# Graph layers and routed experts on one core: work merged around the two graph sums, a selection moved off VectorE, attention items that begin at their first edge

## The chip, the cores and the metric

The kernel runs on one core of a Trainium2 chip. The metric is the device time of one execution in microseconds (us), median of several runs. Everything lies in one launch; all data are float32.

## The reference, cut to what matters

```python
def _layernorm(x): return (x - mean(x)) / sqrt(var(x) + 1e-5)      # rows of 256
...
# x is (6250, 256); 200000 edges sorted by dst, in one of 8 relations each
x = x + relation_layer(_layernorm(x))      # sum over edges of (x @ weight[type])[src] * 0.5**0.5 + h_bias + loop part
x = x + experts(_layernorm(x))             # gates from attention over 131072 + 8192 edges
x = x + selected_layer(_layernorm(x))
x = x + slice_attention(_layernorm(x))     # 8 heads, 64 slices
...
# experts: leaky-relu attention logits, segment softmax over dst, scores, top 2 of 4, softmax
for ei in range(4):
    hh = gelu(x @ W1[ei] + b1[ei])
    out = out + g[..., None] * (hh @ W2[ei] + b2[ei])
...
# selected_layer
h_self, h_neigh = feat @ W_self, feat @ W_neigh
h_sparse = h_neigh with all but the 32 largest of each row at zero
neigh = segment_sum(h_sparse[src], dst) / maximum(deg, 1.0)[:, None]
return h_self + neigh
...
# slice_attention
slice_weights = softmax((x_mid @ W_slice + b_slice) / clip(temperature, 0.1, 5.0))
out_x = slices attended, spread back by slice_weights
return out_x.reshape(B, N, INNER) @ W_out + b_out
```

## The kernel before, in words

The 6250 rows of x lie in SBUF as 49 windows of 128 rows (`b.x`, in the profile `features`, 128x12544 elements). Beside it stands the accumulator `b.acc` (in the profile `big`), 257 columns a window: 256 sums and a count. The program is a row of stages, each a `Phase` with its own code for every engine, closed by a barrier over all engines. Inside a stage engines wait for one another by semaphores only; VectorE (DVE), ScalarE (ACT), TensorE (PE), GpSimd (POOL) and SyncE (SP) run their instructions in the order written. So that order is the whole schedule: nothing is planned at build time.

The stages around the change:

- `relation_sums` (L839) gathers rows of the edges by GpSimd, multiplies them by one-hot places on TensorE and adds the sums on VectorE. `far_edges` does nothing for these inputs.
- `add_relations` (L1585) sets `degree` and adds `acc * 0.5**0.5` (L1602) and the bias `h_bias` (L1606) to x, each in one VectorE instruction over all windows.
- `row_statistics` (L374) of "ln2": 49 `bn_stats` (L397) and a few small steps make mean and rstd.
- `edge_items` (L1974) cuts the sorted attention edges into items of at most 128 edges of one window. It counts per window (L2037, L2039), sums over windows on TensorE (L2074), finds each item's window (L2043, L2045) and tile (L2047), and GpSimd gathers the keys of nine times 128 items (L2023). An item here is an aligned tile of 128 edges together with a window that it touches: a tile on the border of two windows is two items. VectorE then splits the keys (L2055 to L2058), TensorE turns them, and `esrc_items`, `edst_items` and `near_items` are made (L2061 to L2069).
- `attention_inputs`, `far_peaks`, `attention_rows`, and then `attention_edges` (L2105): a turn treats TURN = 8 items. `MAIN` = 848 places for items give 106 turns; the first `UNITS` = 100 turns stand beside one expert unit of TensorE each, the last six stand alone, two of them before a hardware loop, two in it and two behind it. A turn builds one-hot places (L2281), takes the target's terms (L2288), waits for GpSimd's gathers of the sources (L2236), makes logits (L2308) and parts (L2319), and TensorE adds them (L2375). Were there more items than `MAIN`, the flag `a.over` (L2042) would send `far_peaks` (L1736) through its loops over all items and windows.
- `gates` (L2421; its first instruction on VectorE is L2469).
- `blend` (L2529): per window SyncE loads the four experts' outputs (128x4x256, 512 KB) into one of 6 slots, ScalarE makes four diagonals of the gates (L2561), TensorE multiplies each diagonal with an expert's output and sums in PSUM (L2571, `m_mixed`), VectorE adds that to x (L2583) and counts (L2579).
- `sparse_table` (L2592): ScalarE normalizes (L2734) and copies products of both weights out of PSUM into `n_full` (L2754), GpSimd adds the self part to x (L2662), VectorE finds the 32 largest by four rounds of `max` (L2678) and `match_replace` (L2681) over groups of four windows, 8 windows in a ring, and multiplies where the marker stands (L2687) into `n_sparse`, which is stored.
- `neighbour_sums` and `far_edges`, then `add_neighbours` (L2758): the reciprocal of `degree` (L2768), `acc * share` (L2770), its addition to x (L2773), each over all windows; `row_statistics` of "ln4"; `slice_weights` (L2817): loads, TensorE products of two weights, and their scaling by the temperature (L2855, L2861, L2864).
- `slice_tokens`, `slice_attention`, and `slice_output` (L3160): ScalarE copies a window of the slice weights (L3176), TensorE multiplies it (L3185), VectorE adds to x (L3194), SyncE stores.

## Time and profile before

| | us |
|---|---|
| median of 3 runs | 6084.98 (6080.4 to 6094.47) |
| the profiled execution's own time | 6074.39 |
| its span in the profile | 6072.7 |
| TensorE busy | 4259.9 |
| GpSimd busy | 3332.0 |
| VectorE busy | 2604.2 |
| ScalarE busy | 1712.5 |

Where the touched stages lie in the span, by the first and last instruction of their lines:

| stage | from us | to us |
|---|---|---|
| add_relations, ln2, edge_items | 2414.8 | 2492.7 |
| last six attention turns, to the next stage | about 4046 | 4108.2 |
| blend | about 4135 | 4227.9 |
| sparse_table | about 4232 | about 4408 |
| add_neighbours, ln4, slice_weights | 5634.7 | 5712.3 |
| slice_output | 5980.3 | 6072.7 |

A busy share is an average over all stages. What a change to one stage is worth is read from the windows and the timeline of that stage. In a row of the timeline the bracket holds the idle time of the engine just before the instruction and what ended it; "remote" is an event whose source the profile does not name. A row with "xN" stands for N instructions in a row, its duration for all of them.

### The profile page before, as it was taken

The numbers are of one execution on the slowest core, as the hardware profiler recorded it, in microseconds if no ns is written. First come the engines' busy times: TensorE is split into PE (matmuls) and PEld (weight loads), VectorE is DVE, ScalarE is ACT, GpSimd is POOL, SyncE is SP. The second block draws the span as 40 slices with busy tenths as digits, with TensorE's granted clock in tenths as the row PEclk, the third lists the DMA queues.
The fourth block names the chain that finished last, engine by engine and source line by source line (L and its number), as shares of the span: only waits on it lengthen the run. The fifth ranks groups of instructions, "written<-read, shape, count | busy, mean of one in ns | idle before, by whom it ended". The sixth has DMA issues, their size and how long they took to land. (4 is left out here: it accounts for less than half of the span.)

```text
span 6072.7 us, 74083 instructions
## 1 busy us (share of the span) xinstructions
PE 4259.9 (70%) x18413; PEld 3046.3 (50%) x18414; DVE 2604.2 (43%) x8618; ACT 1712.5 (28%) x3921; POOL 3332.0 (55%) x3370
## 2 busy tenths in 40 slices
PE   5888877645555554467777777756668888888498
PEld 2455446333333333445555555545246666666366
DVE  7655424333333332433333333334944443443682
ACT  3344330000000000123333333325365543443132
POOL 5777665666666665055555555551256666666121
PEclk9999998776667766577878888878889999999698
DMA  6444442433333333122222122216144444443001
GB/s 219 154 158 156 158 155 79 130 92 93 91 92 92 92 96 82 14 70 43 43 41 44 40 44 42 42 34 191 41 147 144 138 121 121 121 121 115 16 1 43
DMA packets 331160, 564.00 MB, mean 93 GB/s; under 512 B 75064, under 2 KB 231365, under 8 KB 324507
## 3 DMA queue, kind: packets, MB, share of 16 engines
q0 software_dynamic: 141088, 319.86, 19.9%
q1 hardware_dynamic: 189789, 240.92, 12.6%
q8 instruction: 110, 1.80, 0.1%
q14 instruction: 173, 1.42, 0.1%
HBM read 461.01 MB, written 99.50 MB: 92 GB/s over the span
## 5 line engine op out<-in xcount | busy, mean ns | idle before, releaser
L990 POOL DMA_INDIRECT e_ring<-table,erow x1040 | 990.1, 952 | 523.4 <-issue 267.2
L1290 PE MATMUL e_sums<-e_ring,e_onehot 128*128 128x257 f32 x2080 | 772.2, 518 | 626.6 <-issue 351.5
L2236 POOL DMA_INDIRECT t_source<-source_rows,t_index x848 | 804.3, 948 | 717.9 <-DVE t_parts L2319 476.5
L1401 POOL DMA_INDIRECT e_ring<-table,esrc x800 | 791.2, 989 | 424.2 <-issue 207.3
L1290 PEld LDWEIGHTS e_sums<-e_ring,e_onehot 128*128 128x128 f32 x2080 | 494.0, 257 | 889.9 <-issue 570.8
L585 POOL DMA_INDIRECT r_ring<-rows,esrc x528 | 584.4, 1107 | 239.8 <-issue 131.8
L2395 PE MATMUL t_out<-t_w,t_hidden 128*128 128x256 f32 x1600 | 526.8, 459 | 172.3 <-issue 166.8
L1477 PE MATMUL e_total<-e_loads,e_times 128*128 128x256 f32 x2176 | 577.4, 397 | 47.7 <-issue 36.9
L2395 PEld LDWEIGHTS t_out<-t_w,t_hidden 128*128 128x128 f32 x1600 | 345.6, 225 | 308.6 <-issue 263.1
L1477 PEld LDWEIGHTS e_total<-e_loads,e_times 128*128 128x128 f32 x2176 | 413.3, 198 | 138.6 <-issue 64.7
L1488 PE MATMUL e_sums<-e_ring,e_onehot 128*128 128x256 f32 x1600 | 432.8, 393 | 48.7 <-DMA e_ring<-table,esrc 31.6
L1195 DVE SCALAR_TENSOR_TENSOR big<-e_sums,within,big 128x257 f32 x130 | 63.0, 484 | 875.4 <-DMA r_ring<-rows,esrc 740.9
L2385 PE MATMUL t_raw<-big,t_w 128*128 (+1 forms) x1600 | 426.4, 425 | 7.3 <-issue 5.4
L931 ACT ACTIVATE d_half<-d_keys 128x512 f32<-128x512 f32 x105 | 62.7, 597 | 1204.8 <-issue 614.3
L756 PE MATMUL r_sums<-r_ring,r_onehot 128*128 128x257 f32 x1056 | 300.0, 400 | 134.6 <-DMA r_ring<-rows,esrc 67.6
L742 PE MATMUL r_product<-weights,r_xt 128*128 128x512 f32 x784 | 387.3, 620 | 0.8 <-ACT r_stage L795 0.8
L1424 DVE TENSOR_SCALAR e_place<-e_rampw,ddst 128x512 bf16<-128x512 f32 (+2 forms) x768 | 285.7, 414 | 226.6 <-remote 157.8
L1488 PEld LDWEIGHTS e_sums<-e_ring,e_onehot 128*128 128x128 f32 x1600 | 315.9, 199 | 105.2 <-issue 54.4
L2385 PEld LDWEIGHTS t_raw<-big,t_w 128*128 128x128 f32 x1600 | 334.8, 215 | 61.6 <-issue 10.2
L1382 ACT ACTIVATE e_times<-e_tally 128x512 f32<-128x512 f32 (+2 forms) x384 | 177.8, 463 | 594.1 <-remote 445.9
L756 PEld LDWEIGHTS r_sums<-r_ring,r_onehot 128*128 128x128 f32 x1056 | 196.8, 196 | 286.2 <-issue 180.1
L2281 DVE TENSOR_SCALAR t_place<-t_ramp,near_items 128x128 bf16<-128x128 bf16 x848 | 148.1, 259 | 412.4 <-remote 411.6
(447 smaller groups left out, 6371.8 us busy)
## 6 DMA issues: line engine op xcount, KB each, us to landing
table<-r_stage SPq DMA_DIRECT2D x49, 1024.0 KB
e_loads<-table SPq DMA_DIRECT2D x384, 128.0 KB
t_near<-near_rows SPq DMA_DIRECT2D x106, 256.0 KB
m_outputs<-first_outputs SPq DMA_DIRECT2D x49, 512.0 KB, 4.9
first_outputs<-t_stage SPq DMA_DIRECT2D x96, 256.0 KB
e_ring<-table,erow POOLq DMA_INDIRECT x1040
t_source<-source_rows,t_index POOLq DMA_INDIRECT x848
e_ring<-table,esrc POOLq DMA_INDIRECT x800
```

The costliest lines, as they stand in the source:

```text
L585: eng.indirect_dma_start(ring[:, t % RING, 0:D], None, m["rows1"], bass.IndirectOffsetOnAxis(ap=b.esrc[:, t:t + 1], axis=0)).then_inc(gath ...
L742: mm = eng.matmul(product[n % BANKS][:, :], xt[w % 2][:, k, :], b.weights[:, k, 2 * c:2 * c + 2, :].rearrange("p r o -> p (r o)"), start=( ...
L756: eng.matmul(sums[g % 2][:, 0:ACCW], onehot[t % RING][:, :], ring[:, t % RING, :], start=(t % EGROUP == 0), stop=(t % EGROUP == EGROUP - 1 ...
L990: eng.indirect_dma_start(ring[:, t % BODY, 0:D], None, table, bass.IndirectOffsetOnAxis(ap=b.erow[:, EARLY + t:EARLY + t + 1], axis=0)).th ...
L1290: eng.matmul(sums[g % SUMS][:, 0:ACCW], onehot[t % ONEHOTS][:, :], ring[:, t % BODY, :], start=(t % GROUP == 0), stop=(t % GROUP == GROUP ...
L1401: eng.indirect_dma_start(ring[:, t % BODY, :], None, table, bass.IndirectOffsetOnAxis(ap=b.esrc[:, FROM + t:FROM + t + 1], axis=0)).then_i ...
L1424: eng.tensor_scalar(place[tile % MARKS][:, 0:wide(g) * P], rampw[:, 0:wide(g) * P], b.ddst[:, column(tile):column(tile) + 1], None, ALU.is ...
L1477: mm = eng.matmul(into[:, q, :], times[g % TIMES][:, q * P:(q + 1) * P], loads[:, g % AHEAD, :], start=False, stop=False, skip_group_check ...
L1488: eng.matmul(sums[g8 % 2][:, 0:D], onehot[t % ONEHOTS][:, :], ring[:, s, :], start=(t % GROUP == 0), stop=(t % GROUP == GROUP - 1)).then_i ...
L2236: eng.indirect_dma_start(source[s][:, q, :], None, a.source_rows, bass.IndirectOffsetOnAxis(ap=index[s][:, q:q + 1], axis=0)).then_inc(gat ...
L2385: mm = eng.matmul(raw[g][:, j % 2, :], w1[:, e, k, j * P:(j + 1) * P], b.xt[:, k, bass.ds(w * P, PAIR)], start=(k == 0), stop=(k == KH - 1))
L2395: mm = eng.matmul(out[s][:, q, :], hidden[s][:, j, q * P:(q + 1) * P], w2[:, e, j, :], start=(j == 0), stop=(j == NB - 1))
```

## The change

**Around the first sum.** The bias is loaded in `relation_sums` and added to x there by seven instructions `lift(j)`, one to each run of 7 windows. `add_relations`, the "ln2" statistics and `edge_items` become one stage, `joined_items`: VectorE adds the sums run by run (`join`), counts run by run (`tally`), and the steps of the items stand between.

```diff
+            def lift(j):
+                eng.wait_ge(restored, 16)
+                eng.wait_ge(offset, 16)
+                eng.tensor_tensor(b.x[:, RUN * j:RUN * (j + 1), :], b.x[:, RUN * j:RUN * (j + 1), :],
+                                  bias[:, :].unsqueeze(1).broadcast_to([P, RUN, D]), ALU.add).then_inc(biased, 1)
...
+                if t in bias_at:
+                    lift(bias_at.index(t))
...
+            def join(j):
+                run = b.x[:, RUN * j:RUN * (j + 1), :]
+                eng.scalar_tensor_tensor(run, b.acc[:, RUN * j:RUN * (j + 1), 0:D], 0.5 ** 0.5, run,
+                                         ALU.mult, ALU.add).then_inc(joined, 1)
+            def tally(j):
+                eng.wait_ge(joined, j + 1)
+                for w in range(RUN * j, RUN * (j + 1)):
+                    eng.bn_stats(stats[:, w, :], b.x[:, w, :]).then_inc(tallied, 1)
...
+            join(0)
+            eng.wait_ge(edged, 16)
+            step(eng.tensor_scalar(part[:, :], edge[:, :].bitcast(F32), limit[0:NW, 0:1].bitcast(F32), None, ALU.is_lt))
+            step(eng.tensor_reduce(inner[:, :], part[:, :], AX_X, ALU.add))
+            step(eng.scalar_tensor_tensor(end[:, :], counted[0:NW, 0:1], float(P), inner[:, :], ALU.mult, ALU.add))
+            step(eng.tensor_scalar(laid[:, :], b.ident[0:NW, 0:NW], end[:, 0:1], None, ALU.mult))
...
+            for j in range(EARLIER):
+                join(j + 1)
+                tally(j)
             eng.wait_ge(gathered, 16 * GROUND)
             step(eng.tensor_scalar(word[:, :, :], keys[:, :, :], 8191, None, ALU.bitwise_and))
...
+            for j in range(EARLIER, RUNS):
+                if j + 1 < RUNS:
+                    join(j + 1)
+                tally(j)
...
+            s = Chain(eng, stated)
+            variances(eng, s, b, stats, work)
             eng.wait_ge(turned, 1)
```


VectorE in `joined_items`, before: the two additions, the statistics (49, in a loop), then the items up to the keys' first step (`i_word`).

```order
L1601 TENSOR_SCALAR degree<-big 128x49
L1602 SCALAR_TENSOR_TENSOR features<-big,features 128x12544
L1606 TENSOR_TENSOR features<-features,a_bias 128x12544
L113 UNCONDITIONAL_BRANCH
L391 UNCONDITIONAL_BRANCH
L394 UNCONDITIONAL_BRANCH
L394 ISA
L397 ISA
L397 BN_STATS ln_stats<-features 128x6
```

And VectorE there in the changed kernel, shortly behind the item tiles (`i_tile`, L2120) to the keys' first steps.

```order
L2125 CAST i_windowt<-i_counted 9x128
L2127 TENSOR_TENSOR i_columni<-i_column 9x128
L2073 SCALAR_TENSOR_TENSOR features<-big,features 128x1792
L2079 BN_STATS i_stats<-features 128x6 x7
L2073 SCALAR_TENSOR_TENSOR features<-big,features 128x1792
L2079 BN_STATS i_stats<-features 128x6 x7
L2073 SCALAR_TENSOR_TENSOR features<-big,features 128x1792
L2079 BN_STATS i_stats<-features 128x6 x7
L2073 SCALAR_TENSOR_TENSOR features<-big,features 128x1792
L2079 BN_STATS i_stats<-features 128x6 x7
L2133 TENSOR_SCALAR i_word<-i_keys 128x1152
L2134 CAST i_src<-i_word 128x1152
```


What was ahead of the items' start now stands between the tiles (`i_tile`), which release the gathers, and the keys (`i_word`), which wait for them; run 0 is joined before the tiles, in the wait for the gather of `i_edge`.

**Items begin at a window's first edge.** A window's edges are cut from its own first edge on, not at aligned tiles, so only its last item is short. GpSimd first gathers one row of 128 edges per window (`i_edge`), by which VectorE finds where each window ends; a prefix sum over windows in six doublings gives the items' starts, and the nine gathers of keys use element offsets. `MAIN` becomes 816: 102 turns, of which two stand alone behind the 100 units, in straight code. With the reference's inputs there are 810 items (832 by the old cut).

```diff
-MAIN = -(-(GT * N // GSPACE + NW + 16) // TURN) * TURN
+MAIN = -(-(GT * N // GSPACE + NW // 2 + 10) // TURN) * TURN
...
+            eng.indirect_dma_start(edge[:, :], None, b.sorted, bass.IndirectOffsetOnAxis(
+                ap=whole[:, 0:1], axis=0)).then_inc(edged, 16)
...
             for g in range(GROUND):
-                eng.indirect_dma_start(keys[:, g, :], None, b.sorted, bass.IndirectOffsetOnAxis(
+                eng.indirect_dma_start(keys[:, g, :], None, anywhere, bass.IndirectOffsetOnAxis(
                     ap=tile[:, g:g + 1], axis=0)).then_inc(gathered, 16)
...
+            for k in range(6):
+                reach = 1 << k
+                v.did(eng.tensor_copy(starts[1 - s][:, 0:reach], starts[s][:, 0:reach]))
+                step(eng.tensor_tensor(starts[1 - s][:, reach:NW], starts[s][:, reach:NW], starts[s][:, 0:NW - reach], ALU.add))
+                s = 1 - s
+            start = starts[s]
             v.did(eng.tensor_scalar(a.over[:, :], start[0:1, NW - 1:NW], float(MAIN), None, ALU.is_gt))
             step(eng.tensor_tensor(passed[:, :, :], item[:, :].unsqueeze(2).broadcast_to([P, GROUND, NW]),
...
-            step(eng.tensor_reduce(window[:, :], passed[:, :, :], AX_X, ALU.add))
-            step(eng.tensor_tensor(item[:, :], item[:, :], window[:, :], ALU.subtract))
-            eng.tensor_scalar(tile[:, :], item[:, :], float(GT), None, ALU.min).then_inc(tiled, 1)
...
+            step(eng.tensor_reduce(first[:, :], weighed[:, :, :], AX_X, ALU.add))
+            step(eng.scalar_tensor_tensor(first[:, :], item[:, :], float(P), first[:, :], ALU.mult, ALU.add))
...
-            for t in range(UNITS, LEAD):
-                body(t, t % 2, None, None)
-            with eng.Fori(0, (TURNS - 2 - LEAD) // 2) as i:
-                for n in range(2):
-                    body(2 * i + LEAD + n, (LEAD + n) % 2, None, None)
-            for t in (TURNS - 2, TURNS - 1):
+            for t in range(UNITS, TURNS):
```


**Blend.** VectorE adds the fourth expert (`gate`), one window ahead; ScalarE and TensorE treat three.

```diff
+                wait_if(eng, gated, w - SLOTS + 1)
                 eng.dma_start(outputs[w % SLOTS][:, :, :], first[w]).then_inc(fetched[w % SLOTS], 16)
...
+                for e in range(TURNED):
                     eng.activation(gates[w % BANKS][:, e, :], b.ident[:, :], ACT.Copy,
...
+            def gate(w):
+                eng.wait_ge(fetched[w % SLOTS], 16 * (w // SLOTS + 1))
+                eng.scalar_tensor_tensor(b.x[:, w, :], outputs[w % SLOTS][:, TURNED, :], a.gate[:, w, TURNED:EXPERTS],
+                                         b.x[:, w, :], ALU.mult, ALU.add).then_inc(gated, 1)
...
             for w in range(NW):
+                if w + 1 < NW:
+                    gate(w + 1)
                 eng.wait_ge(summed, w + 1)
+                eng.wait_ge(gated, w + 1)
                 eng.tensor_tensor(b.x[:, w, :], b.x[:, w, :], mixed[w % BANKS][:, 0:D], ALU.add).then_inc(blended, 1)
```


VectorE in the blend, changed kernel (before, a window had L2583 and L2579 alone: the addition of `m_mixed` and the statistics).

```order
L2672 SCALAR_TENSOR_TENSOR features<-m_outputs,gate,features 128x256 x2
L2685 TENSOR_TENSOR features<-features,m_mixed 128x256
L2672 SCALAR_TENSOR_TENSOR features<-m_outputs,gate,features 128x256
L2685 TENSOR_TENSOR features<-features,m_mixed 128x256
L2677 BN_STATS counts<-features 128x6
```


Each window has an instruction more on VectorE, and it stands before the wait for TensorE's sum of the window ahead.

**Selection.** The marker of taken values is now -2^127. VectorE's product is gone; ScalarE's `hide` makes the 0/1 mask from `n_left`, and GpSimd's `choose` multiplies it with `n_full`, both seven windows behind their other work.

```diff
+            def choose(w):
+                eng.wait_ge(masked, w + 1)
+                wait_if(eng, stored[w % WAYS], 16 * (w // WAYS))
+                eng.tensor_tensor(sparse[w % WAYS][:, :], mask[w % WAYS][:, :], full[w % WAYS][:, 1, :], ALU.mult).then_inc(chosen, 1)
...
+                if w >= LATER:
+                    choose(w - LATER)
...
+                            stand(eng, masked, w - WAYS + 1, passed)
+                        eng.match_replace(left[q][:, :], best[q][:, :], values(q), TAKEN).then_inc(picked[q], 1)
                 for w, q in few:
...
-                    eng.scalar_tensor_tensor(sparse[q][:, :], left[q][:, :], LOWEST, full[q][:, 1, :],
-                                             ALU.is_equal, ALU.mult).then_inc(chosen, 1)
+                    eng.sem_inc(searched, 1)
...
+            def hide(w):
+                eng.wait_ge(searched, w + 1)
+                wait_if(eng, chosen, w - WAYS + 1)
+                eng.activation(mask[w % WAYS][:, :], left[w % WAYS][:, :], ACT.Relu, bias=less[:, 0:1],
+                               scale=-2.0 ** -126).then_inc(masked, 1)
...
+                if w >= LATER:
+                    hide(w - LATER)
```


**Around the second sum.** `add_neighbours`, "ln4" and `slice_weights` become one stage: ScalarE multiplies by the degree's share window by window, VectorE adds and counts by runs, then treats the weights; SyncE's loads and TensorE's products lie beside.

```diff
+            eng.wait_ge(shared, 1)
+            for w in range(NW):
+                eng.activation(b.acc[:, w, 0:D], b.acc[:, w, 0:D], ACT.Copy, scale=share[:, w:w + 1]).then_inc(scaled, 1)
...
+            def join(j):
+                run = slice(RUN * j, RUN * (j + 1))
+                eng.wait_ge(scaled, RUN * (j + 1))
+                eng.tensor_tensor(b.x[:, run, :], b.x[:, run, :], b.acc[:, run, 0:D], ALU.add).then_inc(added, 1)
...
+            eng.reciprocal(share[:, :], b.degree[:, :]).then_inc(shared, 1)
+            join(0)
+            for j in range(RUNS):
+                if j + 1 < RUNS:
+                    join(j + 1)
+                count(j)
...
+            s = Chain(eng, stated)
+            variances(eng, s, b, stats, work)
             eng.wait_ge(loaded, 192)
             v.did(eng.tensor_scalar(heat[:, :], heat[:, :], 0.1, 5.0, ALU.max, ALU.min))
```


VectorE in the merged stage, changed kernel, from its start (before: L2768, L2770 and L2773 over all windows, then the statistics, then the weights).

```order
L2992 RECIPROCAL l_share<-degree 128x49
L2984 TENSOR_TENSOR features<-features,big 128x1792 x2
L2989 BN_STATS l_stats<-features 128x6 x7
L2984 TENSOR_TENSOR features<-features,big 128x1792
L2989 BN_STATS l_stats<-features 128x6 x7
```


One addition of a run stands ahead of the statistics of the run before it.

**Output.** The slice weights' softmax is kept per window in the layout that TensorE loads (`f.soft(w)`, partly in `big`), so ScalarE's copies go; the products use 4 PSUM banks in place of 2, and the code is straight where it was a loop. `attt` and `slot` of `slice_attention` share the memory of `meant`.

```diff
                 for q in range(SB):
-                    mm = eng.matmul(product[s][:, 0:D], weight[s][:, q, :], f.outp[:, q, :],
+                    mm = eng.matmul(product[w % BANKS][:, 0:D], f.soft(w)[:, q, :], f.outp[:, q, :],
                                     start=(q == 0), stop=(q == SB - 1))
                 mm.then_inc(multiplied, 1)
-            each_window(eng, body)
```


## Rows read from the trace of the kernel before

**Rows 1.** The page, part 1: busy time of each engine and its share.

```profile
PE 4259.9 (70%) x18413; PEld 3046.3 (50%) x18414; DVE 2604.2 (43%) x8618; ACT 1712.5 (28%) x3921; POOL 3332.0 (55%) x3370
```

**Rows 2.** Windows: us, PE, PEld, DVE, ACT, POOL busy, PEclk, DMA share, GB/s.

```profile
2414.00:2494.00 80.00, 4.66 (x21) 3.97 (x21) 57.70 (x84) 0.24 (x1) 8.92 (x12) 0.52 0.07 20
4228.00:4408.00 180.00, 112.96 (x294) 50.87 (x294) 161.16 (x648) 67.23 (x149) 47.73 (x50) 0.84 0.16 54
```

**Rows 3.** Timeline, 2414 to 2494 us: start, duration, engine, line, operation.

```profile
2414.88 13.22 DVE L1602 SCALAR_TENSOR_TENSOR features<-big,features 128x12544 f32<-128x12544 f32 x1
2442.66 16.10 DVE L397 BATCH_NORM_STATS2 ln_stats<-features  x49 [1.23 <-PEq L116]
2466.15 0.17 DVE L2047 TENSOR_SCALAR i_tile<-i_item 128x9 int32<-128x9 f32 x1
2466.59 0.97 POOL L2023 DMA_INDIRECT i_keys<-sorted_edges,i_tile  x1 [4.50 <-DVE i_tile L2047]
2479.57 0.76 DVE L2055 TENSOR_SCALAR i_word<-i_keys 128x1152 int32<-128x1152 int32 x1 [12.31 <-DMA i_keys<-sorted_edges,i_tile]
2491.30 1.36 DVE L2069 SCALAR_TENSOR_TENSOR near_items<-i_spread,edst_items 128x1152 f32<-128x1152 int32 x1
```

**Rows 4.** Windows, two stretches of 200 us of relation_sums.

```profile
1200.00:1400.00 200.00, 101.31 (x282) 70.59 (x282) 70.84 (x252) 11.95 (x20) 133.42 (x141) 0.71 0.32 93
2200.00:2400.00 200.00, 113.16 (x288) 68.84 (x288) 52.21 (x205) 0.00 (x0) 132.61 (x139) 0.70 0.36 96
```

**Rows 5.** Timeline of VectorE at the end of the attention turns.

```profile
4055.88 0.18 DVE L2308 TENSOR_SCALAR t_logit<-t_leaky 128x32 f32<-128x32 f32 x1
4088.17 1.39 DVE L2281 TENSOR_SCALAR t_place<-t_ramp,near_items 128x128 bf16<-128x128 bf16 x8 [10.43 <-remote]
4103.68 0.18 DVE L2308 TENSOR_SCALAR t_logit<-t_leaky 128x32 f32<-128x32 f32 x1
4108.17 0.36 DVE L2469 TENSOR_TENSOR s_own<-rows,drows 128x196 f32<-128x196 f32 x1 [2.45 <-PEq L116]
```

**Rows 6.** Timeline of the blend, then two windows of it.

```profile
4139.30 35.87 PE L2571 MATMUL m_mixed<-m_outputs,m_gates 128*128 128x256 f32 x153 [32.12 <-DMA m_outputs<-first_outputs]
4143.11 0.42 DVE L2583 TENSOR_TENSOR features<-features,m_mixed 128x256 f32<-128x256 f32 x1 [8.91 <-PE m_mixed L2571]
4227.12 0.75 DVE L2579 BATCH_NORM_STATS2 counts<-features 128x6 f32<-128x256 f32 x2
...
4139.00:4145.00 6.00, 5.70 (x14) 4.59 (x15) 0.42 (x1) 2.18 (x8) 0.00 (x0) 0.54 1.09 351
4160.00:4180.00 20.00, 20.00 (x95) 17.60 (x94) 8.54 (x23) 14.78 (x47) 0.00 (x0) 1.00 0.96 303
```

**Rows 7.** Timeline of sparse_table, then one tile's instructions of two lines.

```profile
4386.58 1.41 DVE L2687 SCALAR_TENSOR_TENSOR n_sparse<-n_left,n_full 128x256 f32<-128x256 f32 x4
4399.44 1.41 DVE L2687 SCALAR_TENSOR_TENSOR n_sparse<-n_left,n_full 128x256 f32<-128x256 f32 x4
...
L2681 DVE MATCH_REPLACE8 n_left<-n_best,n_left x147: 396/397/409, 4250.7 to 4405.0; 128x256 f32<-128x256 f32 x147
L2662 POOL TENSOR_TENSOR features<-features,n_full x49: 722/731/846, 4243.4 to 4387.7; 128x256 f32<-128x256 f32 x49
```

**Rows 8.** Timeline of ScalarE, scaled copies at the program's start.

```profile
39.71 11.40 ACT L259 ACTIVATE features<-features,shift,rstd 128x256 f32<-128x256 f32 x23
```

**Rows 9.** Timeline of VectorE in add_neighbours and slice_weights.

```profile
5635.21 13.23 DVE L2770 TENSOR_TENSOR big<-big,d_share 128x12544 f32<-128x12544 f32 x1
5693.58 0.17 DVE L2855 TENSOR_SCALAR l_heat<-l_heat 128x8 f32<-128x8 f32 x1 [12.52 <-DMA bout<-in_b_out]
5710.43 1.29 DVE L2861 TENSOR_TENSOR wlogit<-l_joined,l_cool 128x512 f32<-128x512 f32 x2 [16.44 <-PE l_bias L2877]
```

**Rows 10.** The chain that ended last: start, us, what.

```profile
5980.27 0.64 ACT o_weight L3176
5980.95 86.54 PE o_product L3185 x392
```

238 lines of the change are left out of this document (147 added, 91 removed).

## The prediction

> **What bounds the kernel now.** I read the page's busy times first: TensorE is busy 70% of the span, GpSimd 55%, VectorE 43% [rows 1]. No engine is full, so a share decides nothing. The program is a row of stages that each end in a barrier over all engines, and the saving of an edit is read inside its stage. The windows view shows which engine fills each stage. In 2414 to 2494 us TensorE works 4.66 us and VectorE 57.70 of 80; in 4228 to 4408 us VectorE works 161.16 of 180 [rows 2]. The timeline of VectorE then shows the order of work and its waits in each touched stage, and the chain that ended last shows what closes the run. A measurement of this kernel tells about 0.2% (12 us) from no change.
>
> **First sum, layer norm and items (joined_items).** Before, VectorE starts at 2414.8 with one addition of 13.22 us over all 49 windows, then one of equal size for the bias, then 16.10 us of 49 statistics from 2442.66, then the items; their first gather issues at 2466.59, and VectorE waits 12.31 us for the last of nine; the last instruction ends at 2492.7 [rows 3]. That is 78 us.
> After, the bias is seven additions of 128x1792 in relation_sums, each a seventh of 13.22 us = 1.89. They stand on VectorE behind whole rounds of that stage. Its pace shows in two stretches of 200 us: VectorE works 70.84 us in one and 52.21 in the other, while GpSimd issues 141 and 139 instructions [rows 4]. 18.6 us more of VectorE moved the pace by nothing one can see, so I cost the lifts at 0. If that cover is missing they cost 7 x 1.89 = 13.2; below nothing is excluded, since they only add.
> What is left in the stage on VectorE: the items' start up to the tile numbers. A 128x9 instruction costs 0.17 us and one of 1152 integers 0.76 [rows 3]; between them I take 0.2 for the thirty small steps and 0.6 for each of the six over 392 to 441 elements. The join of run 0 (1.89) lies inside the wait for the new gather of 49 edge rows, which I take as one issue of 0.97 plus a landing of 3.0. With two trips to TensorE of 0.3 that is 6.0 + 3.6 + 4.0 + 0.6 = 14.2 us to the tile numbers (10 to 18). The nearest rows for the landing are the nine gathers: 2479.57 - 2466.59 = 13.0 us from the first issue to the read of the last keys [rows 3], of which nine issues of 0.97 leave at most 4.3 for landing and gaps. Then four runs of join and statistics, 4 x (1.89 + 2.30) = 16.8 us and 1.1 of columns, cover the nine gathers, which take some 13.5 from the tile numbers, so the wait of 12.31 us goes. Then 3.0 for the four key steps, 10.7 for the remaining two joins and three statistics, 1.25 for the variances, 3.5 for source and near items, 0.5 for the reciprocal and 2.7 for the last two columns. The sum is 14.2 + 1.1 + 16.8 + 3.0 + 10.7 + 1.25 + 3.5 + 0.5 + 2.7 = 53.8, so **-24** (18 to 26). The stall is gone because work lies in it; nothing is late next but VectorE itself.
>
> **Four attention turns fewer.** The first 100 turns lie beside the expert units of TensorE. The last six stand alone: the logits of turn 101 are ready at 4055.88, those of turn 105 at 4103.68, and the next stage's VectorE begins at 4108.17 [rows 5]. The inputs give 810 items where 816 places stand, so turns 102 to 105 have nothing and are dropped. A stall of VectorE in the tail, 10.43 us until 4088.17 by "remote" [rows 5], lies in the dropped piece. From a turn's logits to the next stage it takes 4108.17 - 4103.68 = 4.5 us, so the stage would end at 4055.9 + 4.5 = 4060.4 and not 4108.2: **-47.3** after 0.5 for straight code where a loop was. Lower bound: one 10.43 us stall stays in the last turns, -37. Upper bound: -50.
>
> **Blend.** TensorE now multiplies one expert less. TensorE starts at 4139.30, the first window's sum is at 4143.11 and the last pair of statistics ends at 4227.9 [rows 6]: (4227.1 - 4143.1 - 0.4) / 48 = 1.74 us a window. Eight passes a window become six: 1.74 x 6/8 = 1.30 us. But each window also loads 512 KB. In the first 6 us, when nothing holds the loads back, they move 351 GB/s; in the steady middle 303 GB/s, paced by TensorE [rows 6]. At 351 a window takes 1.50 us, so the loads become the bound: last window lands at 4139.3 + 48 x 1.50 = 4211.3, plus 2.3 us for its product, addition and statistics = 4213.6 against 4227.9: **-14.3**. VectorE has three instructions of 0.42 us in 1.50. If the queue cannot go above 303 GB/s, nothing is won (0). If it can feed 1.30 us, -22. I take 351 because it is this queue's own rate with these tiles.
> The Trainium skill, "DMA: Bandwidth & Descriptors", section "Bandwidth", measures 425 GB/s for a 16 MB load on a core alone. By it the window would take 1.23 us, TensorE would stay the bound at 1.30, and the term would be -22. The trace's 351 is nearer to what this stage does, but it is only 6 us long.
>
> **Selection.** VectorE paces the stage: a group of four windows repeats each 12.86 us (4386.58 and 4399.44), of which the four products that make n_sparse take 1.41 [rows 7]. They go. ScalarE makes a mask instead (one 128x256 row costs 11.40 / 23 = 0.50 us [rows 8]) and GpSimd a product (0.73 us [rows 7]). Both have room in the 180 us: ScalarE works 67.23 and GpSimd 47.73 [rows 2], and they gain 49 x 0.5 = 25 and 49 x 0.73 = 36. New wait: ScalarE's copy of window w stands behind the mask of w-7, which waits until its whole group is searched, so the first window of a group can come late to VectorE. I price it at 0.4 us a group. 12 x (1.41 - 0.4) = 12.1, less 1.6 for the mask, product and store after the last group: **-10.5** (0 to -16).
> The Trainium skill, "GPSIMD Engine Reference", section "Specifications", says that GpSimd shares its SBUF interfaces with VectorE and contends with VectorE instructions of two SBUF inputs. That speaks against more products on GpSimd. The trace: 147 match-and-replace instructions last 396 to 409 ns while GpSimd's additions run among them, though those last 722 to 846 ns [rows 7]. So I add nothing for VectorE; by the page the added products would slow VectorE, within that bound of 0 to -16.
>
> **Second sum, layer norm and slice weights.** Before, from 5634.7: division by the degrees 13.23 us, an equal addition, 16.1 of statistics, then VectorE waits 12.52 us for the last load and 16.44 for the products, and scales these from 5710.43 on [rows 9], the third instruction ending at 5712.3. 77.6 us. After, ScalarE scales 49 windows at 0.50 us [rows 8], VectorE adds a run (1.89) and counts it (2.30), and loads and products lie beside. First run 3.5 us late, 1.6 more for the second, then 13.2 + 16.1 of VectorE, then 1.5 of variances, 0.8 of heat, 2.0 of scaling (1.29 for two [rows 9] and 0.7 for the third), 0.5 for the reciprocal and 0.2 of gaps = 39.4: **-38** (-30 to -40; at -30 ScalarE takes 0.65 an instruction).
>
> **Output.** 392 products run without a gap for 86.54 us, behind one weight copy of 0.64 us by ScalarE [rows 10]. The copies go; TensorE reads the tokens in place. **-0.7** (0 to -1).
>
> **Sum.** -24.0 - 47.3 - 14.3 - 10.5 - 38.0 - 0.7 = -134.8 on the profiled execution's own 6074.39 us (span 6072.7): 5939.6. That execution was 10.6 us under the median of the runs, 6084.98, so on the median's scale the forecast is 5950.2.
>
> **The rivals.**
> 1. *Given back by new waits.* The tail keeps a 10 us stall (-37), the blend stays at 303 GB/s (0), and the ring between ScalarE and GpSimd eats the selection's gain (0). Then -24 - 37 - 38 - 0.7 = -99.7: 5985. For it: three of six terms rest on a rate or a ring that no row shows at the new pace. Chance 0.20 for 5965 to 5990, and 0.06 for 5990 to 6072 (that with late lifts, +13.2, or a slow start of the items).
> 2. *The loads keep up.* The blend runs at TensorE's 1.30 us (-22), the selection loses nothing (-15): 6085 - 24 - 47.3 - 22 - 15 - 38 - 0.7 = 5938. For it: 351 was read while TensorE was just starting. Against: DMA's share is already over 1 in that stretch [rows 6]. Chance 0.12.
> 3. *Slower: one item too many.* If the items pass 816, the flag `over` sends all of them through the slow loops of far_peaks: 1080 turns x 49 windows x 9 small VectorE instructions, each at least the 0.17 us of the smallest row [rows 3], some 81 ms. It decides at the 817th item; the count is 810, so it needs a wrong count. Chance 0.02.
> 4. *The change does not do what it says*: the loads of the blend are issued no earlier, the joins are not interleaved. The order of the changed kernel shows both, so I give it nothing.
>
> **How the numbers follow.** Forecast 5938 to 5965: 0.60; rival 1: 0.20 and 0.06; rival 2: 0.12; slower 0.02. Predicted time 5950. The range 5930 to 5978 takes the forecast, rival 2 and the better half of rival 1, and leaves out 0.2 or less. Faster by over 0.2% (below 6072.8): all but the slower case and 0.01: 0.97.
>
> **What would show it.** VectorE's instructions of joined_items: about 54 us from first to last and no wait over 5 us for the keys. From the last turn's logits to the next stage 4.5 us, and two turns after the units. Sums of the blend 1.50 us apart: 1.30 says rival 2, 1.7 says rival 1. Groups of the selection 11.9 us apart; 12.8 says the ring holds. The merged second stage about 40 us. The relation stage as long as before: 13 us more says that the lifts were not covered. The prediction is wrong if the tail term is below 37, for it is the largest.

## The result and the profile after

The changed kernel takes 5951.1 us, the median of 4 runs (5923.9 to 5955.6), against 6084.5 for the kernel before (4 runs): the ratio is 0.9772, with a 95% interval of 0.9755 to 0.9789. The forecast was 5950, in 5930 to 5978. The profiled execution took 5955.6 us (span 5953.5), 4.5 us above that median; the profiled execution of before was 10.1 us below its own.

The first part of the page, changed kernel. No engine's share has moved much; the gain has to be read stage by stage.

```profile
PE 4277.9 (72%) x18189; PEld 3036.9 (51%) x18190; DVE 2587.9 (43%) x8573; ACT 1705.8 (29%) x3913; POOL 3346.5 (56%) x3389
```

The timeline of VectorE and GpSimd in the first merged stage, changed kernel (columns as in [rows 3]):

```profile
2419.03 2.01 DVE L2073 SCALAR_TENSOR_TENSOR features<-big,features 128x1792 f32<-128x1792 f32 x1
2423.48 0.28 DVE L2094 TENSOR_SCALAR i_part<-i_edge,i_limit 49x128 f32<-49x128 f32 x1 [2.44 <-DMA i_edge<-sorted_edges,i_whole]
2431.19 0.17 DVE L2120 TENSOR_SCALAR i_tile<-i_first 128x9 int32<-128x9 f32 x1
2432.50 2.01 DVE L2073 SCALAR_TENSOR_TENSOR features<-big,features 128x1792 f32<-128x1792 f32 x1
2434.44 2.37 DVE L2079 BATCH_NORM_STATS2 i_stats<-features 128x6 f32<-128x256 f32 x7
2451.57 0.76 DVE L2133 TENSOR_SCALAR i_word<-i_keys 128x1152 int32<-128x1152 int32 x1 [2.10 <-DMA i_keys<-sorted_edges,i_tile]
2472.19 1.36 DVE L2157 SCALAR_TENSOR_TENSOR near_items<-i_spread,edst_items 128x1152 f32<-128x1152 int32 x1
...
2431.65 1.01 POOL L2059 DMA_INDIRECT i_keys<-sorted_edges,i_tile  x1 [9.77 <-DVE i_tile L2120]
2432.97 2.37 POOL L2059 DMA_INDIRECT i_keys<-sorted_edges,i_tile  x1 [0.31 <-issue]
2435.64 0.94 POOL L2059 DMA_INDIRECT i_keys<-sorted_edges,i_tile  x1 [0.30 <-issue]
2436.89 2.67 POOL L2059 DMA_INDIRECT i_keys<-sorted_edges,i_tile  x1 [0.30 <-issue]
```

The wait for the keys is down from 12.31 us [rows 3] to 2.10, but it is not gone: the keys are read 2451.57 - 2431.19 = 20.4 us after the tiles, where it was 2479.57 - 2466.15 = 13.4. Four of the nine gathers are stretched, the second to 2.37 us and the fourth, sixth and eighth to 2.67, where all nine took 0.94 to 0.97 before. The second starts at 2432.97 and ends at 2435.34, 0.8 us after the end of the join that runs from 2432.50 to 2434.51.

The end of the attention turns and the start of the next stage, timeline of VectorE, changed kernel:

```profile
4034.39 0.69 DVE L2414 TENSOR_TENSOR t_stage<-t_out,t_b 128x512 f32<-128x512 f32 x1 [11.90 <-DMA r_xw<-rows]
4042.91 0.18 DVE L2397 TENSOR_SCALAR t_logit<-t_leaky 128x32 f32<-128x32 f32 x1
4047.27 0.36 DVE L2558 TENSOR_TENSOR s_own<-rows,drows 128x196 f32<-128x196 f32 x1 [2.32 <-PEq L117]
```

From the last logits to `s_own` it takes 4.4 us, as before [rows 5], and the turn is the 102nd. VectorE still stands idle for 11.90 us ahead of the logits of the last two turns; the trace of before has 14.74 us at the same place. The blend, timeline of VectorE and a window of 20 us:

```profile
4078.42 0.48 DVE L2672 SCALAR_TENSOR_TENSOR features<-m_outputs,gate,features 128x256 f32<-128x256 f32 x1 [5.11 <-DMA m_outputs<-first_outputs]
...
4122.00 0.41 DVE L2685 TENSOR_TENSOR features<-features,m_mixed 128x256 f32<-128x256 f32 x1
4123.50 0.48 DVE L2672 SCALAR_TENSOR_TENSOR features<-m_outputs,gate,features 128x256 f32<-128x256 f32 x1 [0.75 <-DMA m_outputs<-first_outputs]
4125.02 0.48 DVE L2672 SCALAR_TENSOR_TENSOR features<-m_outputs,gate,features 128x256 f32<-128x256 f32 x1 [0.36 <-DMA m_outputs<-first_outputs]
...
4151.98 0.48 DVE L2672 SCALAR_TENSOR_TENSOR features<-m_outputs,gate,features 128x256 f32<-128x256 f32 x1 [0.30 <-DMA m_outputs<-first_outputs]
...
4104.00:4124.00 20.00, 19.63 (x80) 13.78 (x79) 15.02 (x41) 13.24 (x42) 0.00 (x0) 1.00 1.09 348
```

Where 303 GB/s stood [rows 6], the loads now move 348, and VectorE waits for them. Most windows are 1.50 us apart. The first window's tile and the last one's are used 73.56 us apart, which is 1.53 a window.

The selection, timeline of VectorE, starts of groups of four windows (the second, two in the middle, the last window alone):

```profile
4186.28 1.41 DVE L2796 MAX8 n_best<-n_full 128x8 f32<-128x256 f32 x4
...
4247.26 1.45 DVE L2796 MAX8 n_best<-n_full 128x8 f32<-128x256 f32 x4 [0.74 <-DVE n_left L2801]
4259.21 1.41 DVE L2796 MAX8 n_best<-n_full 128x8 f32<-128x256 f32 x4 [0.29 <-DVE n_left L2801]
...
4319.86 0.43 DVE L2796 MAX8 n_best<-n_full 128x8 f32<-128x256 f32 x1 [0.44 <-DVE n_left L2801]
```

Eleven groups take 4319.86 - 4186.28 = 133.6 us, 12.14 each and not 12.86 [rows 7], and before nearly each group VectorE now has a gap; in the kernel before the four products stood there. The second merged stage, and the first step of the one behind it:

```profile
5557.80 0.47 DVE L2992 RECIPROCAL l_share<-degree 128x49 f32<-128x49 f32 x1 [3.15 <-PEq L117]
5561.23 2.02 DVE L2984 TENSOR_TENSOR features<-features,big 128x1792 f32<-128x1792 f32 x1 [2.97 <-ACT big L2975]
5564.02 2.03 DVE L2984 TENSOR_TENSOR features<-features,big 128x1792 f32<-128x1792 f32 x1 [0.77 <-ACT big L2975]
5594.54 0.68 DVE L3011 TENSOR_TENSOR blogit<-l_bias,l_cool 128x512 f32<-128x512 f32 x1
5603.20 0.69 DVE L3083 TENSOR_TENSOR k_biased<-k_logits,blogit 128x512 f32<-128x512 f32 x1 [7.61 <-PE k_logits L3150]
```

VectorE is through in 37.8 us (its last instruction, a reciprocal, ends at 5595.6), without a wait for loads or products.

The table gives every stretch of the span between the same marks of both profiles, each the start of a VectorE instruction: the second half of the first and of the last addition of sums in relation_sums, the first normalized window after the items, the last logits, `s_own`, the first and last `m_mixed` addition, the first MAX, the instruction behind the last search, the first one-hot (`e_place`) of neighbour_sums, the reciprocal of the degree, `k_biased`, the first and last addition of the output. The last three columns are three experiments, told of below, on another chip; "changed again" is the changed kernel without an edit.

| stretch | before | changed | difference | changed again | best2 | nolift |
|---|---|---|---|---|---|---|
| to the first sum | 914.4 | 910.5 | -3.9 | 834.9 | 828.3 | 833.3 |
| relation_sums | 1495.8 | 1501.5 | +5.7 | 1303.6 | 1306.2 | 1295.8 |
| first join, norm, items | 83.5 | 62.6 | -20.9 | 62.5 | 60.3 | 62.3 |
| attention to the last logits | 1610.0 | 1568.3 | -41.7 | 1129.9 | 1130.5 | 1131.4 |
| from there to `s_own` | 4.5 | 4.4 | -0.1 | 4.3 | 4.4 | 4.3 |
| gates | 34.9 | 34.1 | -0.8 | 34.4 | 34.1 | 33.9 |
| blend | 83.7 | 72.2 | -11.5 | 72.0 | 72.1 | 72.4 |
| to the first MAX | 14.8 | 15.8 | +1.0 | 15.0 | 15.0 | 15.0 |
| selection | 164.2 | 155.4 | -8.8 | 155.4 | 148.9 | 154.8 |
| to neighbour_sums | 4.1 | 5.3 | +1.2 | 5.3 | 5.3 | 5.2 |
| neighbour_sums | 1224.8 | 1227.7 | +2.9 | 1057.1 | 1053.8 | 1052.2 |
| second join, norm, weights | 85.8 | 45.4 | -40.4 | 45.4 | 45.7 | 45.7 |
| slices | 264.1 | 262.1 | -2.0 | 261.9 | 261.7 | 261.2 |
| output | 88.1 | 88.2 | +0.1 | 88.3 | 88.6 | 89.0 |
| span | 6072.7 | 5953.5 | -119.2 | 5070.0 | 5054.9 | 5056.5 |

### The profile page after: what moved, and what is told of

The parts are those of the page before. It is cut to its first block and busy times, and to the rows that moved or that the text cites. A ratio compares the mean times of both kernels' runs of the same rounds, so it can differ in the third digit from the quotient of the medians.

```text
span 5953.5 us, 72825 instructions
## 1 busy us (share of the span) xinstructions
PE 4277.9 (72%) x18189; PEld 3036.9 (51%) x18190; DVE 2587.9 (43%) x8573; ACT 1705.8 (29%) x3913; POOL 3346.5 (56%) x3389
## 5 line engine op out<-in xcount | busy, mean ns | idle before, releaser
L1016 POOL DMA_INDIRECT e_ring<-table,erow x1040 | 996.0, 958 | 523.5 <-issue 250.2
L2325 POOL DMA_INDIRECT t_source<-source_rows,t_index x816 | 771.8, 946 | 701.3 <-DVE t_parts L2408 466.4
L2484 PE MATMUL t_out<-t_w,t_hidden 128*128 128x256 f32 x1600 | 548.0, 478 | 170.8 <-issue 167.8
L2484 PEld LDWEIGHTS t_out<-t_w,t_hidden 128*128 128x128 f32 x1600 | 366.8, 237 | 314.4 <-issue 258.1
L2474 PE MATMUL t_raw<-big,t_w 128*128 (+1 forms) x1600 | 421.2, 421 | 12.0 <-issue 10.5
L2370 DVE TENSOR_SCALAR t_place<-t_ramp,near_items 128x128 bf16<-128x128 bf16 x816 | 143.4, 256 | 435.5 <-remote 430.6
```

The lines of the kernel that those rows point to most:

```text
L1016: eng.indirect_dma_start(ring[:, t % BODY, 0:D], None, table, bass.IndirectOffsetOnAxis(ap=b.erow[:, EARLY + t:EARLY + t + 1], axis=0)).th ...
L2325: eng.indirect_dma_start(source[s][:, q, :], None, a.source_rows, bass.IndirectOffsetOnAxis(ap=index[s][:, q:q + 1], axis=0)).then_inc(gat ...
L2474: mm = eng.matmul(raw[g][:, j % 2, :], w1[:, e, k, j * P:(j + 1) * P], b.xt[:, k, bass.ds(w * P, PAIR)], start=(k == 0), stop=(k == KH - 1))
L2484: mm = eng.matmul(out[s][:, q, :], hidden[s][:, j, q * P:(q + 1) * P], w2[:, e, j, :], start=(j == 0), stop=(j == NB - 1))
```

## The experiments

The runs used several chips, and their times differ: before took 6084 us beside the changed kernel, 5184 in the batch of `serial`, `split`, `load3` and `places848`, 6130 in that of `evac_first`, `defer`, `lift_split` and `best`, and 5179 in that of the last four. So runs are compared in stretches, or with before on the same chip. The stages that do not gather take the same time on all of them: gates, blend, the way to the first MAX, selection, the second merged stage and the output differ by at most 1.6 us where no edit touches them, the slices by 3.2. Of `best`, `best2` and `changed_again` there are five executions each, of every other experiment one; what the gather stages give in a single execution has to be read with care.

**serial**: nothing is joined between tiles and keys.

```diff
-    EARLIER = 4
+    EARLIER = 0
```

> No run is joined or counted between the item tiles and the keys; runs 1 to 6 come behind the keys. Theory A (a gather of GpSimd cannot proceed while VectorE runs a join, an instruction with two SBUF operands): the nine gathers take 0.94 to 1.0 us each and VectorE waits about 12.3 us for the keys. Theory B (the gathers by element offsets are slower in themselves): four or five of them still take 2.4 to 2.7 us and VectorE waits about 19. By either the first merged stage is longer than in the changed kernel, by A 11 us (17.4 us of work no longer cover 13 us of gathers and 6.7 us of stretching goes), by B 17.

Measured: the stage takes 72.6 us, 10.0 more than the changed kernel's. Timeline of GpSimd and VectorE:

```profile
2159.36 0.94 POOL L2059 DMA_INDIRECT i_keys<-sorted_edges,i_tile  x1 [0.30 <-issue]
2168.09 0.94 POOL L2059 DMA_INDIRECT i_keys<-sorted_edges,i_tile  x1 [0.30 <-issue]
2171.43 0.76 DVE L2133 TENSOR_SCALAR i_word<-i_keys 128x1152 int32<-128x1152 int32 x1 [12.46 <-DMA i_keys<-sorted_edges,i_tile]
```

All gathers but the first (1.01) take 0.94 us and VectorE waits 12.46. Theory A holds: it is the join beside it that stretches a gather, not the element offsets. The work between tiles and keys is worth 10 us.

**split**: a join is seven instructions of 128x256, one behind another.

```diff
-                run = b.x[:, RUN * j:RUN * (j + 1), :]
-                eng.scalar_tensor_tensor(run, b.acc[:, RUN * j:RUN * (j + 1), 0:D], 0.5 ** 0.5, run,
-                                         ALU.mult, ALU.add).then_inc(joined, 1)
+                for w in range(RUN * j, RUN * (j + 1)):
+                    eng.scalar_tensor_tensor(b.x[:, w, :], b.acc[:, w, 0:D], 0.5 ** 0.5, b.x[:, w, :],
+                                             ALU.mult, ALU.add).then_inc(joined, 1)
...
-                eng.wait_ge(joined, j + 1)
+                eng.wait_ge(joined, RUN * (j + 1))
```

> Each join of 128x1792 becomes seven of 128x256 (about 0.33 us each back to back, so some 0.3 us more a run). Theory A, with the block held for one instruction at a time: a gather beside joins takes at most 0.94 + 0.4 us, the wait of 2.10 us for the keys is gone, the stage is 1 to 2 us shorter or equal. If the block holds as long as two-operand instructions follow one another: gathers stay at 2.4 to 2.7 us and the stage is 2 us longer. Theory B: as that.

Measured: 65.3 us, 2.7 more. Timelines of GpSimd and VectorE:

```profile
2160.30 3.08 POOL L2059 DMA_INDIRECT i_keys<-sorted_edges,i_tile  x1 [0.30 <-issue]
...
2160.15 2.41 DVE L2073 SCALAR_TENSOR_TENSOR features<-big,features 128x256 f32<-128x256 f32 x7
2162.49 2.37 DVE L2079 BATCH_NORM_STATS2 i_stats<-features 128x6 f32<-128x256 f32 x7
```

The gather begins 0.15 us behind the start of the row of joins and ends 0.8 us behind the row's end. All four rows between tiles and keys hold a gather so (2.78, 3.08, 3.08 and 3.08 us), and the wait for the keys stays at 2.12 us. Splitting does not help here while the pieces follow one another.

**alternate**: with the joins of `split`, the small joins between tiles and keys alternate with the statistics of the run before.

```diff
             for j in range(EARLIER):
-                join(j + 1)
-                tally(j)
+                eng.wait_ge(joined, RUN * (j + 1))
+                for w in range(RUN * j, RUN * (j + 1)):
+                    u = w + RUN
+                    eng.scalar_tensor_tensor(b.x[:, u, :], b.acc[:, u, 0:D], 0.5 ** 0.5, b.x[:, u, :],
+                                             ALU.mult, ALU.add).then_inc(joined, 1)
+                    eng.bn_stats(stats[:, w, :], b.x[:, w, :]).then_inc(tallied, 1)
```

> Between tiles and keys the joins are instructions of 128x256 that alternate with the statistics one by one. If a blocked gather goes on in any gap without a two-operand instruction: each of the gathers takes about twice its time, 1.3 to 1.7 us, all alike; the keys come no earlier (20 us). If it needs only one opening to begin: at most 0.94 + 0.34, the keys come 3 us earlier and the wait of 2.1 is gone. If the blocks add up: 3 us each, the keys come 5 us later or more.

Measured, timelines of GpSimd and VectorE:

```profile
2155.94 1.43 POOL L2059 DMA_INDIRECT i_keys<-sorted_edges,i_tile  x1 [0.31 <-issue]
2157.68 1.02 POOL L2059 DMA_INDIRECT i_keys<-sorted_edges,i_tile  x1 [0.30 <-issue]
2165.62 1.01 POOL L2059 DMA_INDIRECT i_keys<-sorted_edges,i_tile  x1 [0.30 <-issue]
...
2174.01 0.73 DVE L2137 TENSOR_SCALAR i_word<-i_keys 128x1152 int32<-128x1152 int32 x1
```

One opening is enough: the first two gathers take 1.01 and 1.43 us, the others 1.01 to 1.02, and the wait for the keys is gone. The stage is 63.1 us all the same, 0.6 above the changed kernel's, since each run of small joins costs 0.4 us more than a whole one (2.42 against 2.01).

**load3**: the blend loads three of four experts from the seventh window on; the fourth expert's part of the sum is then an older window's.

```diff
-                eng.dma_start(outputs[w % SLOTS][:, :, :], first[w]).then_inc(fetched[w % SLOTS], 16)
+                few = EXPERTS if w < SLOTS else TURNED
+                eng.dma_start(outputs[w % SLOTS][:, 0:few, :], first[w][:, 0:few, :]).then_inc(fetched[w % SLOTS], 16)
```

> From the seventh window on the blend loads three experts' outputs (384 KB) in place of four; the fourth expert's tile keeps an older window, so that part of the sum is left out. Theory: the loads set the blend's pace, at 348 GB/s. Then the windows come 384/512 x 1.50 = 1.13 us apart by the loads, and TensorE's 1.30 (1.727 x 6/8) takes over: the 48 windows take about 63 us and not 72, the stage is 9 to 10 us shorter. Rival: VectorE's chain of three instructions with its waits sets 1.50; then nothing changes.

Measured: the blend takes 63.3 us, not 72.2. A window of 20 us:

```profile
3390.00:3410.00 20.00, 20.00 (x95) 17.61 (x94) 17.57 (x47) 15.05 (x47) 0.00 (x0) 1.00 0.95 300
```

TensorE is busy throughout, a window takes 1.29 to 1.30 us, and VectorE's three instructions keep up. So the loads set the changed blend's pace, and it is 8.9 us above what TensorE would need.

**places848**: 106 turns again.

```diff
-MAIN = -(-(GT * N // GSPACE + NW // 2 + 10) // TURN) * TURN
+MAIN = -(-(GT * N // GSPACE + NW + 16) // TURN) * TURN
```

> The changed kernel with 848 places again, 106 turns, of which the last 38 places are empty. Theory: a lone turn costs its GpSimd gathers and stalls whether or not its places hold an item: 44 to 50 us more, about 12 us for each of four turns. Rival: empty places gather one row again and again or nothing, so the turns are shorter: 20 to 35 us more.

Measured: 1167.8 us of attention beside 1128.6 to 1129.6 in the three other runs of that batch, with 102 turns: 39 us for four turns. Timeline of VectorE:

```profile
3359.13 0.22 DVE L2397 TENSOR_SCALAR t_logit<-t_leaky 128x32 f32<-128x32 f32 x1
3369.14 0.18 DVE L2397 TENSOR_SCALAR t_logit<-t_leaky 128x32 f32<-128x32 f32 x1
3373.64 0.36 DVE L2558 TENSOR_TENSOR s_own<-rows,drows 128x196 f32<-128x196 f32 x1 [2.45 <-PEq L117]
```

The expected band was 44 to 50 and the rival's 20 to 35; the run falls between. An empty turn costs 10 us like a full one, which is eight gathers at 0.95 + 0.30 us. On the first chip the dropped turns took 47.8 us, 12 each, with the stall of 10.43 us of [rows 5] among them; in this run VectorE has no such stall before `t_place`. That the stalls are the whole difference is read from these rows, not tested.

**evac_first**: ScalarE copies a window before it makes the mask of the window seven back.

```diff
-                if w >= LATER:
-                    hide(w - LATER)
                 eng.wait_ge(multiplied, w + 1)
...
                                ACT.Copy).then_inc(evacuated, 1)
+                if w >= LATER:
+                    hide(w - LATER)
```

> In the selection's stage ScalarE copies a window out of PSUM before it makes the mask of the window seven back, in place of after it. Theory R (the ring: VectorE's gaps of 0.29 and 0.79 us between groups are waits for ScalarE's copies): both gaps go, the stage is 5 to 6 us shorter. Theory S (the gaps come from VectorE's own queue, which waits for the end of its last replacement, adds to the semaphore and then starts the next group, and at each second group goes round a loop): nothing changes, within 1 us.

Measured: 155.9 us of selection, against 155.4, and the gaps are still there (0.74 and 0.28 us). Theory R falls: the gaps of VectorE are no waits for ScalarE's copies.

**defer**: with the edit of `evac_first`, VectorE tells of a group behind the next group's first MAX.

```diff
+            def tell(few):
+                for w, q in few:
+                    eng.wait_ge(picked[q], (w - q) * (2 * ROUNDS // WAYS) + 2 * ROUNDS)
+                    eng.sem_inc(searched, 1)
...
                         eng.max(best[q][:, :], values(q)).then_inc(picked[q], 1)
+                    if r == 0:
+                        tell(previous)
```

> As the run before, and VectorE tells of a searched group only behind the first four MAX of the next group. Theory S: the gap of 0.29 us goes and of the 0.79 some 0.3 goes (the loop's branch stays), 12 groups: the stage is 3.5 to 6 us shorter than in the changed kernel. Theory R: no more than the run before gave.

Measured: 148.0 us of selection, 7.4 less than the changed kernel and 7.9 less than `evac_first` on the same chip. Timeline of VectorE, two groups:

```profile
4275.44 1.41 DVE L2801 MAX8 n_best<-n_full 128x8 f32<-128x256 f32 x4
4286.95 1.42 DVE L2801 MAX8 n_best<-n_full 128x8 f32<-128x256 f32 x4
```

11.51 us a group, with no gap. Theory S holds. It gave more than the 3.5 to 6 us expected, since the longer gap, at the loop, goes too.

**lift_split**: each bias addition as seven instructions of 128x256.

```diff
-                eng.tensor_tensor(b.x[:, RUN * j:RUN * (j + 1), :], b.x[:, RUN * j:RUN * (j + 1), :],
-                                  bias[:, :].unsqueeze(1).broadcast_to([P, RUN, D]), ALU.add).then_inc(biased, 1)
+                for w in range(RUN * j, RUN * (j + 1)):
+                    eng.tensor_tensor(b.x[:, w, :], b.x[:, w, :], bias[:, :], ALU.add).then_inc(biased, 1)
...
-            eng.wait_ge(biased, RUNS)
+            eng.wait_ge(biased, NW)
```

> Each addition of the bias in the relation stage (128x1792, 2.0 us) becomes seven of 128x256, one behind another. Theory A (a gather waits until the two-operand instruction that runs on VectorE ends, one instruction at a time): the seven gathers of 1.76 to 2.75 us fall to below 1.4, GpSimd's 8.4 us of stretching to 1 to 3. The stage's length by its own pace: the same within 3 us, or up to 8 us shorter if GpSimd sets it there. If the block holds for a whole row of such instructions: they stay above 1.7.

Measured: two of the seven rows of additions hold a gather to their end (2.57 and 2.76 us); beside the other five the gathers take 0.94 to 1.15 us. One row of each kind, timelines of GpSimd and VectorE:

```profile
1686.71 1.15 POOL L1016 DMA_INDIRECT e_ring<-table,erow  x1 [0.30 <-issue]
1686.63 2.42 DVE L1243 TENSOR_TENSOR features<-features,e_bias 128x256 f32<-128x256 f32 x7
...
1758.88 2.76 POOL L1016 DMA_INDIRECT e_ring<-table,erow  x1 [0.30 <-issue]
1758.39 2.43 DVE L1243 TENSOR_TENSOR features<-features,e_bias 128x256 f32<-128x256 f32 x7
```

All 1040 gathers of the stage together take 992.1 us, where they take 996.0 to 999.6 in the runs with whole additions. But in `best`, which has the same split additions, three rows hold a gather (up to 3.34 us) and the sum is 998.2. So split additions let some gathers through and hold others, and what decides it stays open. The stage's length does not tell either: 1510.7 us here, 1504.2 in `best`, beside 1507.3 and 1506.0 with whole additions on that chip.

**nolift**: the calls of `lift` are left out, the bias is missing.

> The seven additions of the bias are left out, so that h_bias is missing from the output. Theory A prices them at 8.4 us of GpSimd's time in the relation stage. If GpSimd's row of gathers sets that stage's pace where they stand (1660 to 1735 us), the stage is 5 to 9 us shorter than in the changed kernel's run; if TensorE or the ring of sums takes it up, it is the same within 3 us.

Measured: relation_sums takes 1295.8 us, beside 1303.6 in `changed_again` and 1303.0 to 1306.2 in all seven runs with the whole additions that have before at 5179 to 5184 us. The groups of GpSimd's gathers in that stage, first of `changed_again`:

```profile
L1016 POOL DMA_INDIRECT e_ring<-table,erow x1040 | 997.1, 959 | 316.8 <-issue 241.6 <-PE e_sums L1325 75.2
```

and of `nolift`:

```profile
L1016 POOL DMA_INDIRECT e_ring<-table,erow x1040 | 989.6, 952 | 316.9 <-issue 240.7 <-PE e_sums L1322 76.2
```

The gathers are busy 7.5 us less and idle as long, and the stage is 7.8 us shorter (7.2 to 10.4 against each of the seven): the additions cost what they stretch.

**best**: `split`, `lift_split`, `defer`, and ScalarE's wait for GpSimd's constant put before the first mask.

> Split joins, split additions of the bias, masks behind the copies, the searched groups told late, and ScalarE does not wait for GpSimd's constant before the first norms of the selection's stage (-1.0 us). By theories A and S: 1 to 2 + 0 to 3 + 4 to 6 + 1 = 6 to 12 us less than the changed kernel, 5939 to 5945 on the scale of its median 5951; against before about 0.9758. If only S holds: 5 us less.

Measured: 6005.3 us (median of 5), ratio 0.9794 (0.9765 to 0.9822) to before on its chip. The expected ratio was 0.9758. The changed kernel was not run there, so this does not rank the two. By stretches it gains 7.4 us in the selection and gives 3 back in the first merged stage (65.5), not the 6 to 12 expected; the moved wait gives nothing that shows (15.0 to the first MAX, where others have 14.2 to 15.8).

**changed_again** and **best2**, on one chip in the same rounds. `best2` is the changed kernel with `defer` and

```diff
-    EARLIER = 4
+    EARLIER = 5
```

> The changed kernel itself, beside the next one on the same chip. Its ratio to before again 0.977 within 0.002; its relation stage beside the one of the kernel without the additions of the bias.

> The changed kernel with two edits: the searched groups are told late with masks behind the copies (7.4 us on the selection's stage in the run before), and five runs in place of four are joined and counted before the keys (the wait of 2.10 us goes; the additions of the bias and the joins stay whole). Expected 9 to 10 us less than the changed kernel on the same chip, ratio to before 0.9755. Rival: the fifth run stretches one more gather or uncovers the wait for the turned keys behind, then 7 us less.

Measured: before 5178.6, `changed_again` 5071.7 (5070.3 to 5078.9), ratio 0.9799 (0.9785 to 0.9812); `best2` 5061.2 (5056.4 to 5066.3), ratio 0.9775 (0.9762 to 0.9788). `best2` is 10.5 us faster than the changed kernel, and their runs do not overlap: -6.5 in the selection, -2.2 in the first merged stage, whose wait for the keys is gone; the rest lies in stretches that the edits do not touch. It is the faster of the two versions that were run five times each on one chip. The changed kernel's ratio is a little above the expected band: it gains 106.9 us here and 133.4 on the first chip. 9 us of that difference are the dropped turns, 39 us and not 48; the rest stays open, as no profile of before was taken on this chip.

## Why the prediction was right

**The sum** came out at -133.4 between the medians, against -134.8, and at -119.2 between the two profiled executions. The terms as measured below add up to -122: -20.9 + 7.8 - 47.9 - 12.3 - 6.6 - 40.4 - 1.9. So the mechanisms of the large terms were right, but that the medians meet the forecast to 1.4 us is luck: some 11 us of that gain are in no term that a run accounts for. How far the gather stages stray shows in the attention, which took 1577.6 to 1586.8 us in four runs on one chip, with the same code there.

**The first merged stage: -20.9, forecast -24.** The steps up to the tiles were sized right: 14.3 us from the first small step (2417.03) to the tiles, with 14.2 in the sum. The step that failed is "cover the nine gathers, which take some 13.5": beside joins they took 20.4, from the tiles to the keys, so 2.1 us of wait stayed. `best2` takes it away with a fifth run ahead of the keys, 2.2 us. The last 1 us is spread: a start 0.4 us later, behind GpSimd's `iota` instructions, and runs of join and statistics of 4.2 us and a little more in place of 4.19.

**The additions of the bias: +8, forecast 0.** This is the step that was wrong. The argument compared VectorE's load in two stretches and found cover. But GpSimd had none: it goes from one gather to the next with 0.30 us between, and each addition holds one up. `nolift` gives 7.8 us; the bound in the text was 13.2. The comparison was of another kind of work: of the 70.84 us of VectorE in the first stretch of [rows 4], 32.7 are two-operand sort steps on `d_keys`, which lies in PSUM, and none of the 140 gathers there takes over 1.05 us. Where both operands of a sort step lie in SBUF, as in the program's first stage (`r_keys`), the trace of before already shows a stretched gather:

```profile
303.88 0.68 DVE L456 TENSOR_TENSOR r_keys<-r_keys 128x512 f32<-128x512 f32 x1
304.48 0.68 DVE L457 TENSOR_TENSOR r_keys<-r_keys 128x512 f32<-128x512 f32 x1
304.00 1.98 POOL L585 DMA_INDIRECT r_ring<-rows,esrc  x1 [0.30 <-issue]
```

**The attention turns: -47.9 by the marks of the tail** (4108.17 - 4055.88 = 52.29 before, 4047.27 - 4042.91 = 4.36 now), forecast -47.3. The 102 turns up to there took 6.1 us longer, within what one code strays. `places848` shows what is general in it: 10 us a turn.

**The blend: -12.3, forecast -14.3.** The bound was named rightly, about 1.50 us a window by the loads at 348 GB/s; `load3` shows it. By the ends that the prediction used, from TensorE's first product to the last statistics, the stage takes 76.3 us (4078.44 to 4154.7) where 74.3 were forecast and 88.6 stood: -12.3. The start was right, 31.2 us behind `s_own` as before (31.1). Mis-sized were the 48 windows, 73.6 us between first and last and not 72.0, and the last window's tail, 2.7 us and not 2.3. The 425 GB/s of the Trainium skill, "DMA: Bandwidth & Descriptors", section "Bandwidth", are not reached here; the trace's 351, read over 6 us, was the better guide.

**The selection: -6.6 in all, forecast -10.5.** The mechanism given for the loss, ScalarE's copies late by the ring, is refuted by `evac_first`. The gaps are VectorE's own: its queue waits for the last replacement before it adds to the semaphore and begins the next group. A group without the products would take 12.86 - 1.41 = 11.45 us; it takes 12.14, and 11.51 in `defer`. So 0.7 us a group is lost where 0.4 was allowed, over 12 groups 3.5 us more, and that makes most of the miss. That the allowance came near is luck, as it was made for another cause. 1.0 us more lies ahead of the first MAX, which single runs do not separate from their spread (14.2 to 15.8 where no edit touches it). The 1.2 behind the search, where mask and product follow the last window, had been allowed for with 1.6.

**GpSimd beside VectorE.** The prediction set the rule of the Trainium skill, "GPSIMD Engine Reference", section "Specifications", against the match-and-replace rows and found no contention. For those rows that stands: GpSimd's new products take 0.72 to 0.74 us each. But the rule speaks of two SBUF inputs, which a match-and-replace on one 128x256 tile does not have, and the joins and bias additions do. `serial`, `split`, `alternate` and `nolift` agree with it, with the side of the cost turned: GpSimd waits (2.37 to 3.08 us a gather), while a join takes 2.0 us with a gather beside it or without. So does the sort on `d_keys`, with one operand in PSUM, beside which gathers take 0.94 to 0.95. The rule was weighed in the wrong stage.

**The second merged stage: -40.4, forecast -38.** Right; ScalarE starts the first run 3.0 us late and the second 0.8, the sum had 3.5 and 1.6.

**Output: +0.1 in its own stretch, -2.0 in the one before**, where the first weight copy lay, forecast -0.7. The slices take 261.2 to 264.4 us in the runs that leave them alone, so this small term cannot be told from no gain.

Of rival 1's three losses two did not come, the blend at 303 GB/s and a stall kept in the tail; of the third, the selection's gain, 3.9 of 10.5 us were lost and not all. Rival 2 did not come, as the loads stayed at 1.50 us a window. Rival 3 did not arise.

## What to carry to other kernels

When work is moved into the cover of another stage, ask which engine paces that stage, and whether the moved instruction holds that engine up: cover on its own engine is not enough. Long VectorE instructions with two operands in SBUF cost a row of GpSimd gathers up to their own length; alternating them with one-operand work gives the gathers an opening, cutting them up alone may not. A row that shows cover has to show it for the same kind of instruction: here the sort on PSUM held no gather up and the additions in SBUF did. Signal the end of a group behind the first instructions of the next, if the queue has to wait for a result before it can signal.
